# A transformer layer's attention in one 64x64 matmul tiling, the lower rows' matmuls behind the upper rows'

## What is computed

```python
xn = _layernorm(x, axis=-1)                  # x: 8 x 2048 x 1024
q, k, v = xn @ Wq.T, xn @ Wk.T, xn @ Wv.T    # 16 heads of 64
attn = einsum('bqhd,bkhd->bhqk', q, k) * 64**-0.5 * pmask
s = softmax(attn) @ v
Wq1, Wq2 = _quantize(W1), _quantize(W2)      # clip(round(W / (mean|W| + 1e-5)), -1, 1)
g = _silu(relu(xn @ Wq1.T + b1) @ Wq2.T + b2)   # 1024 -> 4096 -> 1024
return x + s * g
```

## Time and profile before

| | us |
|---|---|
| median of 3 runs | 969.94 |
| lowest, highest | 969.58, 1115.1 |
| profiled execution | 968.92 |
| its span, slowest core | 967.3 |
| spans of the 8 cores | 965.1 to 967.3 |
| granted clock of the cores | 0.998 to 1.000 |

### The profile page before, as it was taken

How to read it: one execution, slowest core, us unless ns; L and a number is a source line. 1 busy time by engine, 2 the same in 40 slices (tenths; PEclk the granted TensorE clock), 3 DMA queues, 4 the chain that set the end, 5 groups by cost and what they waited for, 6 DMA issues and landing times.

```text
span 967.3 us, 32593 instructions; the slowest of 8 cores (965.1 to 967.3 us)
## 1 busy us (share of the span) xinstructions
PE 930.9 (96%) x12524; PEld 380.1 (39%) x12524; DVE 758.8 (78%) x1095; ACT 627.5 (65%) x739; POOL 27.4 (3%) x54
## 2 busy tenths in 40 slices
PE   2899999999999999999999999999999999999997
PEld 1443333333333333333333333333333333444443
DVE  3858879997788888888888888888788888732568
ACT  2566776777777777777777777777777775033322
POOL 0000000000000000000000000000000000100500
PEclk9999999999999999999999999999999999999999
DMA  8588696663110111121112110201110111631785
GB/s 211 145 228 258 238 297 207 228 222 113 35 45 26 44 47 46 45 46 45 28 43 46 46 46 25 62 30 46 35 46 25 45 46 46 170 114 66 207 286 183
DMA packets 30710, 100.71 MB, mean 104 GB/s; under 512 B 3680, under 2 KB 3680, under 8 KB 30304
## 3 DMA queue, kind: packets, MB, share of 16 engines
q1 hardware_dynamic: 20800, 75.56, 24.7%
q0 software_dynamic: 5152, 14.68, 7.4%
q10 hardware_dynamic: 4608, 8.39, 2.4%
HBM read 96.52 MB, written 8.39 MB: 108 GB/s over the span
## 4 chain that ended last, share of the span: by engine, by line
PE 86%; DVE 5%; DMA 4%; issue 3%; ACT 1%; DVEq 0%; SPq 0%; ACTq 0%
PE PS L342 41%; PE PS L472 14%; PE PS L456 13%; PE PS L338 11%; PE PS L371 3%; PE PS L490 2%; DMA arena<-xP 2%; DMA outT<-arena 2%; PE PS L413 2%; DVE arena L747 1%; ACT arena L560 1%; PE PS L404 1%; DVE arena L718 1%; DVE arena L683 0%; DVE arena L707 0%
## 5 line engine op out<-in xcount | busy, mean ns | idle before, releaser
L560 ACT ACTIVATE arena<-PS 128x1024 bf16<-128x1024 f32 x512 | 496.0, 1021 | 195.5 <-PE PS L456 195.5
L342 PE MATMUL PS<-arena 128*32 128x512 bf16 x7552 | 448.6, 379 | 1.1 <-DVE arena L667 1.1
L342 PEld LDWEIGHTS PS<-arena 128*32 128x32 bf16 x7552 | 203.2, 97 | 204.1 <-issue 1.8
L456 PE MATMUL PS<-arena 64*128 64x512 bf16 x1024 | 155.7, 381 | 2.8 <-ACT arena L560 2.6
L472 PE MATMUL PS<-arena 128*32 128x512 bf16 x2048 | 157.6, 384 | 0.3 <-DVE arena L707 0.3
L338 PE MATMUL PS<-arena 128*128 128x512 bf16 x672 | 151.2, 379 | 0.0
L713 DVE TENSOR_TENSOR arena<-arena 128x1024 bf16<-128x1024 bf16 x200 | 136.3, 681 | 0.4 <-ACT arena L560 0.4
L702 DVE SCALAR_TENSOR_TENSOR arena<-arena 128x1024 bf16<-128x1024 f32 x64 | 82.2, 1284 | 34.4 <-PE PS L338 24.8
L338 PEld LDWEIGHTS PS<-arena 128*128 128x128 bf16 x672 | 65.6, 98 | 79.3 <-issue 0.7
L667 DVE TENSOR_SCALAR arena<-PS,arena 128x512 bf16<-128x512 f32 x96 | 71.5, 746 | 17.6 <-PE PS L342 16.8
L718 DVE TENSOR_TENSOR arena<-arena 128x1024 bf16<-128x1024 bf16 x100 | 69.0, 690 | 7.8
(11 more groups left out here) (51 smaller groups left out, 447.3 us busy)
## 6 DMA issues: line engine op xcount, KB each, us to landing
arena<-w1b SPq DMA_DIRECT2D x16, 1024.0 KB, 7.2
arena<-w1b SPq DMA_DIRECT2D x32, 512.0 KB, 3.7
arena<-w2b SPq DMA_DIRECT2D x16, 1024.0 KB, 7.4
arena<-w2b SPq DMA_DIRECT2D x32, 512.0 KB, 3.5
arena<-xP SPq DMA_DIRECT2D x16, 512.0 KB, 4.9
arena<-xT POOLq DMA_DIRECT2D x32, 256.0 KB, 10.0
outT<-arena ACTq DMA_DIRECT2D x32, 256.0 KB, 4.1
arena<-wvb POOLq DMA_DIRECT2D x2, 1024.0 KB, 14.8
```

The lines of the kernel that those rows point to most:

```text
L342: mm = e.matmul(out[32 * q:32 * q + 32, :], stationary[:, c * 128 + 32 * q:c * 128 + 32 * q + 32], moving[c], start=(first and c == 0), st ...
L456: mm = e.matmul(bank(b + hh), kb[hp % 2][rows, kc * 128:(kc + 1) * 128], rhs, start=True, stop=True, tile_position=(64 * hh, 0))
L560: e.activation(out=pt[gi % PR][:], in_=PS[:, b:b + 1024], func=AF.Exp, scale=0.125, bias=-4.0).then_inc(a_exp, 1)
```

## The change

All matmuls of the attention stage are cut into tiles of 64 rows by 64 columns. The upper 64 rows (r = 0) and the lower 64 rows (r = 1) each have a stream of their own: for units, weighted values and denominators both halves add into the same bank, and the lower half comes several steps behind the upper; for the scores, r is the head. Each step issues two upper and two lower matmuls. Exponentials are now one per head and window instead of one per chunk. Units (F1, F2, Q, K, V, THR) and the denominators D of a pass take turns in banks 5, 6 and 7, with the ring `RING`; weighted values lag two windows. Sums of two and of four are made by VectorE in all passes, and the denominators of a pass are 4 steps in one window (g % 8 == 2). The denominators come out on all 128 partitions, so the folding and the copies are gone, and logarithm and reciprocal are one instruction each, 128 x 512. ScalarE evicts V units and many F1 units. VectorE evicts two windows later, takes the absolute sums in halves of 1024 columns, and quantises in two parts (`below`, `above`) in different windows. THR moves from windows 23 and 56 to 20 and 56 and takes no slot; the feed-forward units start at window 24 instead of 25, and the tail has 77 units instead of 79.

```diff
 XR = 4
-PR = 6
-TR = 6
-NRAW = 7
+PR = 3
+AR = 6
...
-THR_SLOT = (23, 56)
-FFN_FROM = 25
+THR_AT = (20, 56)
+FFN_FROM = 24
...
+def den_at(g):
+
+    return g // 8 - 1 if g >= 10 and g % 8 == 2 else None
...
+RING = list(PRE)
+for _g in range(NGR):
+    if den_at(_g) is not None:
+        RING.append(("D", den_at(_g)))
+    if _g in THR_AT:
+        RING.append(("THR", THR_AT.index(_g)))
+    if SLOT[_g] is not None:
+        RING.append(SLOT[_g])
+UNITS = [u for u in RING if u[0] != "D"] + TAIL
...
+RBANKS = (5, 6, 7)
...
+BANK = {u: RBANKS[n % 3] for n, u in enumerate(RING)}
...
+PREV = {u: RING[n - 3] for n, u in enumerate(RING) if n >= 3}
...
+for _g in range(NGR):
+    if SLOT[_g] is not None and SLOT[_g][0] == "V":
+        ON_ACT.add(SLOT[_g])
+    if SLOT[_g] is not None and SLOT[_g][0] == "F1" and _g % 8 != 1 and (_g < THR_AT[1] or SLOT[_g][3] % 2 == 1):
+        ON_ACT.add(SLOT[_g])
...
+        def eight_half(r, u, stationary, moving):
+
+            rows = slice(64 * r, 64 * r + 64)
+            for c in range(8):
+                for m in range(2):
+                    mm = e.matmul(bank(BANK[u])[64 * m:64 * m + 64, :], stationary[c][rows, 64 * m:64 * m + 64],
+                                  moving[c][rows, :], start=(r == 0 and c == 0), stop=(r == 1 and c == 7),
+                                  tile_position=(64 * r, 64 * m))
+                if c == 7:
+                    mm.then_inc(p_u if r == 1 else p_hu, 1)
+                yield c == 7
...
+        def scores(r, g):
...
+            if g >= 1:
+                e.wait_ge(a_exp, 2 * g - 1 + r)
...
+            for k in range(2):
+                for m in range(2):
+                    col = (2 * j + k) * 128 + 64 * m
+                    mm = e.matmul(bank(2 * r + k)[64 * m:64 * m + 64, :], kb[hp % 2][rows, col:col + 64], rhs,
+                                  start=True, stop=True, tile_position=(64 * r, 64 * m))
+                if k == 1:
+                    mm.then_inc(p_s[r], 1)
+                yield False
...
+        def den(r, itp):
+...
+            for k in range(4):
+                for hh in range(2):
+                    mm = e.matmul(bank(BANK[u])[64 * hh:64 * hh + 64, :], ones[rows, :],
+                                  aq[(4 * itp + k) % AR][rows, 512 * hh:512 * hh + 512],
+                                  start=(r == 0 and k == 0), stop=(r == 1 and k == 3), tile_position=(64 * r, 64 * hh))
+                if k == 3:
+                    mm.then_inc(p_d if r == 1 else p_hu, 1)
+                yield k == 3
...
+        def upper(w):
+
+            if den_at(w) is not None:
+                yield from den(0, den_at(w))
+            if w >= 2:
+                yield from pv(0, w - 2)
+            if w < NGR:
+                yield from scores(0, w)
+                if SLOT[w] is not None:
+                    yield from unit_half(0, SLOT[w])
+
+        def lower_attention(w):
+
+            if w < NGR:
+                yield from scores(1, w)
+            else:
+                yield False
+                yield False
+            if w >= 2:
+                yield from pv(1, w - 2)
+
...
 
         e.wait_ge(v_c, 3)
-        for g in range(NGR):
-            scores(g)
-            if g >= 1:
-                pv(g - 1)
-            for n in DEN_AT.get(g, []):
-                den(n)
-            if SLOT[g] is not None:
-                unit(SLOT[g])
-        pv(NGR - 1)
+        ring = lower_ring()
+        ended = []
+        taken = 0
+        inside = False
+        now = 0
+        for w in range(NGR + 2):
+            first = 4 if den_at(w) is not None else 0
+            if w in THR_AT:
+                ended.append(now)
+            up, low, p = upper(w), lower_attention(w), 0
+            while True:
+                end = next(up, None)
+                if end is None and p >= first + 6:
+                    break
+                if end:
+                    ended.append(now)
+
+
+                if first + 2 <= p < first + 6:
+                    next(low, None)
+                elif inside or (taken < len(ended) and now > ended[taken] + 2):
+                    inside = not next(ring)
+                    taken += not inside
+                p, now = p + 1, now + 1
...
-        def exps(gi):
-            b = 1024 * (gi % 2)
-            e.wait_ge(p_s, gi + 1)
-            if gi >= PR:
-                e.wait_ge(p_pv, gi - PR + 1)
-...
-            e.activation(out=pt[gi % PR][:], in_=PS[:, b:b + 1024], func=AF.Exp,
+        def exps(r, g):
+            e.wait_ge(p_s[r], g + 1)
+            if r == 0 and g >= PR:
+                e.wait_ge(p_pv, 2 * (g - PR) + 2)
+                e.wait_ge(v_t, g - PR + 1)
+            e.activation(out=pt[g % PR].rearrange("p (k h c) -> p k h c", k=2, h=2)[:, :, r, :],
+                         in_=PS[:, 1024 * r:1024 * r + 1024].rearrange("p (k c) -> p k c", k=2), func=AF.Exp,
                          scale=0.125, bias=-4.0).then_inc(a_exp, 1)
 
         def ln_den(itp):
-            e.wait_ge(v_d, itp + 1)
-            e.activation(out=lnd[0:64, :], in_=lnd[0:64, :], func=AF.Ln).then_inc(a_ln, 1)
-
-        def recip(itp, hh):
+            e.wait_ge(p_d, itp + 1)
+            e.activation(out=lnd[:], in_=bank(4 if itp == NITP - 1 else BANK[("D", itp)]),
+                         func=AF.Ln).then_inc(a_ln, 1)
+
+        def recip(itp):
             e.wait_ge(a_ln, itp + 1)
             if itp >= 1:
                 e.wait_ge(v_s, itp)
-            e.activation(out=rcp[64 * hh:64 * hh + 32, :], in_=lnd[32 * hh:32 * hh + 32, :], func=AF.Exp,
-                         scale=-1.0).then_inc(a_rc, 1)
-
-        for g in range(NGR):
-            exps(2 * g)
-            exps(2 * g + 1)
-            if g >= 8 and g % 8 == 2:
+            e.activation(out=rcp[:], in_=lnd[:], func=AF.Exp, scale=-1.0).then_inc(a_rc, 1)
...
+        for g in range(NGR + 2):
+            if g >= 2 and SLOT[g - 2] in ON_ACT:
+                out_of_psum(SLOT[g - 2])
+            if g >= 11 and g % 8 == 3:
                 ln_den(g // 8 - 1)
-            if g >= 8 and g % 8 in (3, 4):
-                recip(g // 8 - 1, g % 8 - 3)
+            if g < NGR:
+                exps(0, g)
+                exps(1, g)
...
         def tile_sum(g):
+
+            n = g // 2
             e.wait_ge(a_exp, 2 * g + 2)
...
-            e.tensor_tensor(out=tt[g % TR][:], in0=pt[(2 * g) % PR][:], in1=pt[(2 * g + 1) % PR][:],
-                            op=ALU.add).then_inc(v_t, 1)
-
-        def four_sum(g):
-            e.wait_ge(v_t, t_at(g + 1))
-            e.tensor_tensor(out=tt[g % TR][:], in0=tt[g % TR][:], in1=tt[(g + 1) % TR][:],
-                            op=ALU.add).then_inc(v_f, 1)
-
...
+            if g % 2 == 0 and n >= AR:
+                e.wait_ge(p_d, (n - AR) // 4 + 1)
+            if g % 2 == 1 and g >= 3:
+                e.wait_ge(v_f, n)
+            e.tensor_tensor(out=(odd if g % 2 else aq[n % AR])[:], in0=pt[g % PR][:, 0:1024],
+                            in1=pt[g % PR][:, 1024:2048], op=ALU.add).then_inc(v_t, 1)
+
+        def four_sum(n):
+
+            e.wait_ge(v_t, 2 * n + 2)
+            e.tensor_tensor(out=aq[n % AR][:], in0=aq[n % AR][:], in1=odd[:], op=ALU.add).then_inc(v_f, 1)
 
         def attended(itp):
             hp, qs = itp // TS, itp % TS
-            e.wait_ge(a_rc, 2 * itp + 2)
-            for hh in range(2):
-                e.tensor_copy(out=rcp[64 * hh + 32:64 * hh + 64, :],
-                              in_=rcp[64 * hh:64 * hh + 32, :]).then_inc(v_rc, 1)
-            e.wait_ge(v_rc, 2 * itp + 2)
+            e.wait_ge(a_rc, itp + 1)
...
-        for g in range(NGR + 1):
-            done = SLOT[g - 1] if g >= 1 else None
-            if done is not None:
-                out_of_psum(done)
-            if g >= 8 and g % 8 == 0:
+        for g in range(NGR + 2):
+            if g - 2 in THR_AT:
+                out_of_psum(("THR", THR_AT.index(g - 2)))
+            if g >= 2 and SLOT[g - 2] is not None and SLOT[g - 2] not in ON_ACT:
+                out_of_psum(SLOT[g - 2])
+            if 1 <= g <= NGR:
+                tile_sum(g - 1)
+            if 2 <= g <= NGR and g % 2 == 0:
+                four_sum(g // 2 - 1)
+            if g >= 9 and g % 8 == 1:
                 numerators(g // 8 - 1)
-            if g > 8 * NRAW:
-                tile_sum(g - 1)
-            if g >= 8 and g % 8 == 1:
-                denominators(g // 8 - 1)
-            if g >= 8 and g % 8 == 6:
+            if g >= 13 and g % 8 == 5:
                 attended(g // 8 - 1)
-            if g >= 8 * NRAW + 2 and g % 2 == 0:
-                four_sum(g - 2)
+            if below_at(g) is not None:
+                below(below_at(g))
+            if above_at(g) is not None:
+                above(above_at(g))
             for i in GAM_AT.get(g, []):
                 absolute_sum(i)
-            if done in F_OF and quant_after(F_OF[done]) is not None:
-                quantise(quant_after(F_OF[done]))
```

437 lines of the change are left out of this document (221 added, 216 removed).

## The result

The changed kernel takes 1092.8 us (median of four runs, 1091.9 to 1094.2) against 969.94: a ratio of 1.127, 95% interval 1.125 to 1.129. The forecast was 978 with a range to 1003, so it was wrong by 115 us, and the time lies 90 us beyond the slowest rival (D, 1003). The profiled execution has a span of 1091.3.

A forecast was written before the change was run, and what follows sets the result against it. Bounds: VectorE in the first 56 windows, the exchange with ScalarE in later plain windows. 69.6 + 172 + 584 + 3 + 147.7 = 976.3 us of span, plus 1.6, taken as 978 us; range 944 to 1003.

The forecast's parts named there:

- Rival D: VectorE falls behind around denominators, 1 us each group, early only 92% busy (180 us): 1003 us, chance 0.13.
- The lower denominators end one step ahead of the scores: Window after the denominators: ScalarE's logarithm starts early, delays the exponentials by some 0.25 us; window 2.97 us.
- A V or F1 unit's lower half ... ends in the same step ahead of the scores: ScalarE's evictions in attention: exponentials some 0.2 to 0.35 us late; late stage 34 x 0.21 = 7 us.
- The exchange with ScalarE: Plain windows: scores and exponentials wait on each other in a loop of 2.69, taken as 2.72 us, above TensorE's 2.59.
- rival A: Attention windows: the exchange does not bind, since the upper exponential can start early; 928 us, chance 0.07.
- The 64x64 step: TensorE in attention: a step of four 64x64 matmuls takes 0.216 us, far bound 0.27.
- C: TensorE in attention: the 64x64 step is longer, through weight loads or doubled bank writing; at 0.24, 1001 us; chance 0.13.
- E: TensorE in attention: the two 0.11 us pauses stay, as waits for weights after a semaphore; 983 us, chance 0.07.
- Eight late windows: Last 200 windows: 3.46 + 2.97 + 6 x 2.72 = 22.75 us per eight, 569 in all, plus 7 evictions and 8 banks.
- The early stage: First 56 windows: VectorE is the bound, 169.5 us of work, taken as 172 us.
- The tail: Behind attention: two units move into attention, three more steps for the last denominators; 150.5 becomes 147.7 us.
- half used steps: Start and end of attention: the lag of the lower rows leaves some 14 steps half used, 3 us.

The follow-up runs named there:

- a1: Changed kernel, but the one-column threshold matmul no longer takes a step of the lower stream: 1002.8 us, ratio 1.034 to the kernel before.
- a2: a1, and in window 2 the lower stream issues two steps of its units for one: 982.7 us, ratio 1.013 to the kernel before.
- a5: a2 with each lower step one place later in TensorE's queue: 977.6 us, ratio 1.008 to the kernel before.
- a8: a2 with a lower half let in as soon as its upper half has ended: 977.6 us, ratio 1.008 to the kernel before.
- a7: a5 with a lower half let in as soon as its upper half has ended: 966.9 us, ratio 0.997 to the kernel before.
- a10: a7 with a lower half let in one step after its upper half has ended: 968.2 us, ratio 0.997 to the kernel before.

## Why the prediction was wrong

- **The step that failed:** "The lower denominators end one step ahead of the scores" and "A V or F1 unit's lower half ... ends in the same step ahead of the scores". True for windows 24 to 55 of 256 (a lower half ends at p = 1), elsewhere the end is at p = 6 or 7, four steps or more behind the start of the scores. I read one place of the order, found the last two steps of a lower unit ahead of the scores there, and took it for all. I had priced the logarithm at 0.25 us and an eviction at 0.21; with the end at p = 6 or 7 a window with one of them takes 3.3 to 4.15 us in place of 2.7, 0.6 to 1.4 us more, and the window with denominators, which wants a bank, 4.4 in place of 3.5. A third wait on the lower half had no term in my sum at all: the queries for the next pass, whose late eviction makes the last window of a pass 3.6 in place of 2.8. By the runs: 90 us late (a1) and 20 early (a2) of the 115.
- **The exchange with ScalarE,** forecast 2.69 to 2.72: measured 2.71 in plain windows. That its cause is the second upper pair behind the lower pair's wait is borne out by a2 against a5 (2.71 and 2.59) and a8 against a7 (2.73 and 2.62). So rival A (it does not bind) was out for this kernel.
- **The 64x64 step,** taken as 0.216: right. Twelve steps are 2.59 us (a10), sixteen 3.46. C and E are out: no window is longer by its steps, and no pauses of 0.1 us are left between L534, L377 and L509.
- **Eight late windows,** forecast 22.75, with 8 + 7 us for banks and evictions 584 for the stage: 575.6 with the position put right (a2). Eight such windows take 22.9, so the allowances of 15 were too high by half.
- **The early stage,** forecast 172 by VectorE's load of 169.5: the load was 160 and the stage 184.4 with the position put right. Rival D had 180 for it by the mechanism that is seen there, VectorE behind and TensorE waiting for it; I gave it 0.13.
- **The tail,** forecast 147.7, and 3 for half used steps: 150.3, and 150.5 in a2.
- **The range** was built from prices of mechanisms that I had in view. What was missing was a rival on the schedule itself: "a lower half ends later than in the place I looked at". It had a price in the same rows: 0.15 to the scores, 5 steps of 0.216, 0.58 from the last step to the eviction, 0.69 for the eviction and 1.94 for the exponentials make an estimate of 4.44 us for a window with an eviction, against 4.15 measured.
